# Twelve gathered table rows laid by VectorE, and the last tile's last three tables gathered in two halves

## The chip, the core and the metric

The kernel runs on one core of a Trainium2 chip. The metric is the device time of one execution in microseconds. Before the change it is 101.78 us, the median of three runs (101.72 to 101.84).

## The reference

A recommendation tower for 512 samples: 26 tables are looked up, all pairs of the 27 vectors (the dense one and 26 rows) are multiplied, and three layers follow.

```python
e = jnp.stack([tbl_0[ids[:, 0]], ..., tbl_25[ids[:, 25]]], axis=1)       # 512 x 26 x 128
combined = jnp.concatenate([dense_features[:, None, :], e], axis=1)      # 512 x 27 x 128
interactions = jnp.einsum('bnd,bmd->bnm', combined, combined)
z = jnp.concatenate([dense_features, interactions[:, _TRIU_I, _TRIU_J]], axis=1)
h = jnp.concatenate([z, dense_features], axis=1)                         # 512 x 607
h = jnp.maximum(h @ W_top1 + b_top1, 0.0)                                # 512 wide
h = jnp.maximum(h @ W_top2 + b_top2, 0.0)                                # 256 wide
y = h @ W_top3
```

## The kernel before

The samples are cut into four tiles of 128 (t = 0 to 3 in the code; the text counts tiles from 1). The kernel collects all 27 vectors of every sample in `xt`, with the 128 features on the partitions, `[128, sample/2, 27, 2]`.

Eleven small tables (1000 rows) are not gathered: TensorE multiplies them, in two parts, with a one-hot matrix that VectorE and ScalarE make (`lookup`, L339), and ScalarE copies the result to `xt`. This fills the first 47 us, beside the gathers.

The other fifteen tables are gathered by GpSimd: one indirect DMA fetches the rows of one table for the 128 samples of one tile into `rows_sb` (L312), samples on the partitions. Sixty such gathers follow one another, counted 0 to 59 here, fifteen a tile. `GROUPS` bundles them: four groups (4, 4, 4 and 3 tables) in each of tiles 1 to 3, and five (4, 4, 4, 2, 1) in tile 4, so groups 0 to 16. `rows_sb` holds two tiles; a gather of tile 3 or 4 waits until the group that had its place is turned (`FREED_BY`). Up to gather 42 every third one also waits for a lookup (L311), which keeps the gathers from running ahead.

When a group has landed, TensorE transposes its tables one by one into PSUM (`turn_group`, L354: a matrix product with the identity, 128 columns a table), and ScalarE copies the group to `xt` (`copy_group`, L697). Groups 0 to 7 are turned between the lookups (`AFTER_LOOKUP`), the others at places written out by hand in TensorE's program (L492 to L555).

Then, for each tile: `gram` (L376) makes the 27 x 27 products of each sample, in four quarters of 32 samples, `ps_gram`; `pack` on VectorE (L602, L607) transposes them in blocks of 32 and packs the triangle; `turn_z` (L387), ScalarE's `copy_z`, `layer1_dense` (L415) and `layer1_pairs` (L425), the ReLU on ScalarE (lower half, L720) and on VectorE (upper half, L638), `layer2` (L439), `layer3` (L468). The last tile has a version in chunks (`pack_last`, `turn_last_z`, `layer1_last_pairs` L402, `layer2_last`). TensorE's program mixes a tile's products with the layers of the tile before. `gram(3, 0)` waits until all groups are copied.

SyncE issues the loads: first the row numbers of all tiles for the gathers (`ids_sb`, L276), on which GpSimd's first gather waits, then tables and weights.

Of the kernel before, what the change touches and what calls it, by code (L numbers as in the profile page):

```python
# [15 lines left out]
P = 128  # L16
B = 512
# [60 lines left out]
assert all(sum(sizes) == len(GATHERED) for sizes in SIZES_OF_TILE)  # L78
FREED_BY = {g: max(e for e, (s, j, m) in enumerate(GROUPS) if s == t - ROWS_RING and j < i + k)
            for g, (t, i, k) in enumerate(GROUPS) if t >= ROWS_RING}  # L80

AFTER_LOOKUP = [[], [], [], [0], [1], [2], [3], [4], [5], [6], [7]]
LOOKED_UP_BESIDE = sum(len(gs) for gs in AFTER_LOOKUP)
assert sum(AFTER_LOOKUP, []) == list(range(LOOKED_UP_BESIDE)) and len(AFTER_LOOKUP) == FIRST_HALF_UP_TO
GROUPS_UP_TO = [sum(t <= tile for t, _, _ in GROUPS) for tile in range(TILES)]
# [41 lines left out]
def build(nc, dense_by_column, ids, ids_by_table, tables, w1, w2, columns, identity, out):  # L127
    with ExitStack() as ctx:  # L128
# [3 lines left out]
        def sem(name):  # L132
            return ctx.enter_context(nc.semaphore(name))
# [8 lines left out]
        ids_sb = sb("ids_sb", [P, TILES, F], I32)  # L142
        dense_sb = sb("dense_sb", [D, B], F32)
# [33 lines left out]

        ids_landed = sem("ids_landed")
        ident_landed = sem("ident_landed")
# [18 lines left out]
        group_copied = sem("group_copied")  # L198
        gram_done = sem("gram_done")
# [38 lines left out]

        def last_z(c):

            return ps_gram[:, c - 1, 0:P] if c else ps_z[:, 0, 0:P]
# [18 lines left out]
        def _(sp):  # L260
# [33 lines left out]
        def _(pool):  # L294
# [7 lines left out]
            pool.wait_ge(ids_landed, 16)  # L302
            for g, (t, first, n) in enumerate(GROUPS):
                if t >= ROWS_RING:
                    pool.wait_ge(group_turned, FREED_BY[g] + 1)
                for k in range(first, first + n):
                    f = GATHERED[k]
                    issued = t * len(GATHERED) + k
                    if issued >= GATHERS_AHEAD and (issued - GATHERS_AHEAD) % GATHERS_PER_LOOKUP == 0:
# [3 lines left out]
                        rows_sb[:, t % ROWS_RING, k, :], None, tables[f],  # L313
                        bass.IndirectOffsetOnAxis(ids_sb[:, t, f:f + 1], 0),
                    ).then_inc(group_landed[g], 16)

        @block.tensor
        def _(pe):
# [26 lines left out]
            def turn_group(g):  # L345

                t, first, n = GROUPS[g]
                if g >= 2:
                    pe.wait_ge(group_copied, g - 1)
                if g == 0:  # L350
                    pe.wait_ge(ident_landed, 16)
                pe.wait_ge(group_landed[g], 16 * n)
                for slot in range(n):
                    last = pe.transpose(ps_rows[:, g % 2, slot * P:(slot + 1) * P],  # L354
                                        rows_sb[:, t % ROWS_RING, first + slot, :], ident)
                last.then_inc(group_turned, 1)

            def gram(t, quarter):
# [4 lines left out]
                if quarter == 0:  # L363

                    pe.wait_ge(group_copied, GROUPS_UP_TO[t])
# [4 lines left out]
                    else:  # L370
                        pe.wait_ge(blocks_turned, t)
                for s in range(first, first + SPQ):
                    for j in range(P // NPAD):
                        b = t * P + j * NPAD + half * SPB + s
# [117 lines left out]
            turn_group(8)  # L492
# [4 lines left out]
            turn_group(9)  # L497
# [8 lines left out]
            layer2(0, 1)  # L506
            turn_group(10)
            turn_group(11)
# [7 lines left out]
            turn_group(12)  # L516
# [7 lines left out]
            turn_group(13)  # L524
# [3 lines left out]
            turn_group(14)  # L528
# [4 lines left out]
            turn_group(15)  # L533
            turn_group(16)
            layer1_pairs(2, 3)
            gram(3, 0)
            gram(3, 1)
            layer3([0, 1])
            layer2(2, 0)
            layer1_dense(3, 0)  # L540
# [106 lines left out]

# [178 lines left out]
```

## Time and profile before

| what | us |
|---|---|
| time, median of three runs | 101.78 |
| time of the profiled execution | 102.27 |
| its span, first to last instruction | 100.5 |
| TensorE busy (products) | 94.2 |
| VectorE busy | 52.6 |
| ScalarE busy | 50.6 |
| GpSimd busy | 61.3 |
| the sixty gathers, busy | 60.9 |

PE is TensorE's products, PEld its weight loads, DVE VectorE, ACT ScalarE, POOL GpSimd, SP SyncE. A gather's busy time on POOL is the time in which GpSimd issues it; its data land later. Times in the profile's answers are microseconds from the start of the span.

### The profile page before, as it was taken

To read this page: it belongs to the slowest core of one execution; us is meant where nothing else is said; L and a number is where in the kernel's file an instruction comes from. 1 tells how busy PE (TensorE), PEld (TensorE's weight loads), DVE (VectorE), ACT (ScalarE), POOL (GpSimd) and SP (SyncE) were. 2 spreads that over 40 slices of the span, in tenths; PEclk is the share of its full clock that TensorE was granted. 3 is DMA by queue.
4 is the path that set the end of the run, shared out by engine and by line. 5 is a ranking of instruction groups with operands and counts; after the bars stand their busy time and mean duration, and the time that the engine had idled before them with its cause. 6 is when DMAs were issued, how large, how long until landed. Compare 5 with 4: busy or idle time off the path is not lost.

```text
span 100.5 us, 3478 instructions
## 1 busy us (share of the span) xinstructions
PE 94.2 (94%) x1525; PEld 77.6 (77%) x1525; DVE 52.6 (52%) x117; ACT 50.6 (50%) x84; POOL 61.3 (61%) x66
## 2 busy tenths in 40 slices
PE   5999999999999999999999989999999897998990
PEld 1347788668888888899888878898898795987970
DVE  4599959999999969975000610262022601126020
ACT  2888999897499299384211242007400543003521
POOL 1488877777778877777777777777777760000000
PEclk9999999999999999999999999999999999999999
DMA  2999999999999999512222222212122221000000
GB/s 55 243 325 257 299 281 277 258 249 278 238 264 265 268 328 373 162 52 59 52 59 52 59 52 62 59 52 59 52 59 59 52 52 26 7 7 0 7 0 1
DMA packets 5366, 13.46 MB, mean 134 GB/s; under 512 B 1732, under 2 KB 1992, under 8 KB 5223
## 3 DMA queue, kind: packets, MB, share of 16 engines
q1 hardware_dynamic: 3260, 9.11, 33.0%
q0 software_dynamic: 1920, 3.94, 14.8%
q8 instruction: 12, 0.20, 0.9%
q10 hardware_dynamic: 170, 0.18, 0.8%
q14 instruction: 4, 0.02, 0.1%
HBM read 13.23 MB, written 0.00 MB: 132 GB/s over the span
## 4 chain that ended last, share of the span: by engine, by line
POOL 55%; issue 19%; PE 14%; DMA 8%; POOLq 1%; ACT 0%
POOL rows_sb L312 55%; DMA rows_sb<-tbl,ids_sb 5%; PE ps_a L402 3%; PE ps_gram L376 3%; DMA ids_sb<-ids 2%; PE ps_h L439 2%; PE ps_h L468 1%; POOLq L128 1%; PE ps_rows L451 1%; PE ps_rows L354 1%; PE ps_a L415 1%; PE ps_rows L456 1%; PE ps_a L425 1%; ACT y_sb L741 0%; PE ps_gram L395 0%
## 5 line engine op out<-in xcount | busy, mean ns | idle before, releaser
L312 POOL DMA_INDIRECT rows_sb<-tbl,ids_sb x60 | 60.9, 1015 | 20.4 <-issue 17.1
L339 PE MATMUL ps_a<-onehot,part_sb 125*128 125x512 f32 (+1 forms) x208 | 45.0, 366 | 0.4 <-ACT part_sb L668 0.2
L339 PEld LDWEIGHTS ps_a<-onehot,part_sb 125*128 125x128 f32 x208 | 34.1, 188 | 8.2 <-DVE onehot L575 1.2
L575 DVE TENSOR_SCALAR onehot<-idrow,row_id 125x1024 fp32r<-125x1024 int16 (+1 forms) x41 | 26.6, 708 | 1.5 <-DMA idrow<-ids_by_table 1.5
L584 DVE TENSOR_TENSOR part_sb<-table_sb,part_sb 125x512 fp32r<-125x512 f32 x22 | 14.4, 683 | 2.7 <-ACT part_sb L668 2.6
L690 ACT COPY xt<-ps_a 128x512 f32<-128x512 f32 (+1 forms) x13 | 7.6, 584 | 13.7 <-PE ps_a L339 13.5
L697 ACT COPY xt<-ps_rows 128x512 f32<-128x512 f32 (+3 forms) x17 | 9.9, 584 | 8.6 <-PE ps_rows L354 8.6
L376 PE MATMUL ps_gram<-xt 128*27 128x27 f32 x1024 | 13.4, 195 | 0.5 <-issue 0.2
L376 PEld LDWEIGHTS ps_gram<-xt 128*27 128x27 f32 x1024 | 11.1, 108 | 3.3 <-issue 0.6
L638 DVE TENSOR_SCALAR table_sb<-ps_a,columns_sb 128x128 f32<-128x128 f32 x8 | 2.4, 346 | 20.4 <-PE ps_a L425 17.3
L668 ACT CAST part_sb<-table_sb 125x1024 fp32r<-125x1024 f32 (+1 forms) x12 | 11.7, 979 | 0.6 <-DMA table_sb<-tbl 0.6
L602 DVE STREAM_TRANSPOSE table_sb<-ps_gram 128x864 f32<-128x864 f32 x3 | 3.3, 1084 | 13.7 <-PE ps_gram L376 13.7
L354 PE MATMUL ps_rows<-ident_sb,rows_sb 128*128 128x128 f32 x60 | 9.3, 274 | 1.2 <-DMA rows_sb<-tbl,ids_sb 1.2
L425 PE MATMUL ps_a<-table_sb,w_sb 128*128 128x128 f32 x72 | 9.4, 280 | 0.2 <-ACT table_sb L704 0.2
L354 PEld LDWEIGHTS ps_rows<-ident_sb,rows_sb 128*128 128x128 f32 x60 | 7.1, 141 | 2.4 <-ACT xt L697 1.0
L425 PEld LDWEIGHTS ps_a<-table_sb,w_sb 128*128 128x128 f32 x72 | 8.5, 192 | 0.5 <-issue 0.4
L679 ACT ACTIVATE distance<-idrow,row_id 125x1024 f32<-125x1024 int16 (+1 forms) x7 | 7.7, 1094 | 0.3 <-DMA idrow<-ids_by_table 0.3
L684 ACT ACTIVATE onehot<-distance 125x1024 fp32r<-125x1024 f32 (+1 forms) x7 | 7.0, 1001 | 0.5
L439 PE MATMUL ps_h<-table_sb,w_sb 128*128 128x128 f32 x48 | 6.9, 288 | 0.0
L439 PEld LDWEIGHTS ps_h<-table_sb,w_sb 128*128 128x128 f32 x48 | 5.8, 191 | 0.4 <-issue 0.2
L476 PE MATMUL ps_z<-zeros 128*128 128x512 bf16 x13 | 4.6, 529 | 1.2 <-DVE zeros L559 1.2
L736 ACT ACTIVATE table_sb<-ps_h,columns_sb 128x128 f32<-128x128 f32 x6 | 1.9, 373 | 5.6 <-PE ps_h L439 5.6
(41 smaller groups left out, 43.3 us busy)
## 6 DMA issues: line engine op xcount, KB each, us to landing
table_sb<-tbl SPq DMA_DIRECT2D x11, 448.0 KB
idrow<-ids_by_table SPq DMA_DIRECT2D x5, 256.0 KB, 7.5
w_sb<-w SPq DMA_DIRECT2D x1, 1280.0 KB, 9.9
rows_sb<-tbl,ids_sb POOLq DMA_INDIRECT x60, 5.7
table_sb<-tbl SPq DMA_DIRECT2D x10, 52.0 KB
w_sb<-w SPq DMA_DIRECT2D x1, 512.0 KB, 9.6
dense_sb<-dense_by_column SPq DMA_DIRECT2D x1, 256.0 KB, 7.6
idrow<-ids_by_table ACTq DMA_DIRECT2D x1, 128.0 KB, 2.8
```

The source lines that it names most:

```text
L312: pool.indirect_dma_start(rows_sb[:, t % ROWS_RING, k, :], None, tables[f], bass.IndirectOffsetOnAxis(ids_sb[:, t, f:f + 1], 0),).then_inc ...
L339: last = pe.matmul(ps_a[:, i % 2, a:b], parts_sb[part][:, w, c * D:(c + 1) * D], unit_onehot(u, c)[:, member, a:b], start=(part == HIGH an ...
L354: last = pe.transpose(ps_rows[:, g % 2, slot * P:(slot + 1) * P], rows_sb[:, t % ROWS_RING, first + slot, :], ident)
L376: last = pe.matmul(ps_gram[j * NPAD:j * NPAD + N, half, s * N:(s + 1) * N], x, x, start=True, stop=True)
L425: last = pe.matmul(h1_block(t, m), w1_sb[:, c, m * P:(m + 1) * P], zt[:, t % 2, c, :], start=False, stop=(c == ZC - 1), skip_group_check=True)
L439: last = pe.matmul(h2_block(t, m), w2_sb[:, k, m * P:(m + 1) * P], h1[:, t % 2, k, :], start=(k == 0 and m == 0), stop=(k == M1 - 1), skip ...
L575: dve.tensor_scalar(unit_onehot(u, c), idrow[0:VP, w, 0:n, :], row_id[0:VP, first + c:first + c + 1], None, ALU.is_equal).then_inc(onehot_ ...
L584: dve.tensor_tensor(parts_sb[LOW][:, w, columns], table_sb[0:VP, s, columns], parts_sb[HIGH][:, w, columns].bitcast(F32), ALU.subtract).th ...
L668: act.copy(parts_sb[HIGH][:, w, first:end], table_sb[0:VP, s, first:end]).then_inc(part_ready[HIGH], 1)
L679: act.activation(distance[:, 0:n, :], idrow[0:VP, w, 0:n, :], ACT.Abs, bias=row_id[0:VP, negated:negated + 1]) \
L690: act.copy(xt[:, a // RUN:b // RUN, 1 + h, :], ps_a[:, i % 2, a:b].rearrange("p (q r) -> p q r", r=RUN)).then_inc(lookup_copied, 1)
L697: act.copy(xt[:, t * P // RUN:(t + 1) * P // RUN, slots, :].rearrange("p q n r -> p n q r"), ps_rows[:, g % 2, 0:n * P].rearrange("p (n q ...
```

## The change

Three parts. **Laying:** tile 2 (code t = 1) is now bundled 4, 3, 8 and tile 4 again 4, 4, 4, 3. Two groups, `LAID`, are not turned by TensorE: group 6 (the last eight tables of tile 2) and group 11 (the first four of tile 4) are transposed by VectorE from `rows_sb` straight into `xt`, in 32 x 32 blocks, sixteen instructions each (`lay_group`). Twelve tables leave TensorE and ScalarE. **Halves:** the last three tables of tile 4 are gathered for its first 64 samples (group 14, three gathers of 64 rows) and then for the other 64 (group 15, three more, with their row numbers in a tensor of their own, and into rows of `rows_sb` that group 7 leaves free). `gram` of the last tile takes the first 64 samples in quarters 0 and 1, the others in quarters 2 and 3, and `copy_last_z` puts the samples back in order. TensorE's program at the end is written in another order. **Row numbers:** those of tile 1 are loaded first, the rest in a second transfer. Groups in after number 0 to 15.

```diff
-LAST_GROUP_SIZES = [4, 4, 4, 2, 1]
-SIZES_OF_TILE = [GROUP_SIZES] * (TILES - 1) + [LAST_GROUP_SIZES]
+SIZES_OF_TILE = [GROUP_SIZES, [4, 3, 8], GROUP_SIZES, GROUP_SIZES]
...
+HALF_TILE = P // 2
+FIRST_HALVES = len(GROUPS) - 1
+SECOND_HALVES = len(GROUPS)
+GROUPS.append(GROUPS[FIRST_HALVES])
+HALVED = GATHERED[-GROUP_SIZES[-1]:]
+FREES_ROWS = 7
...
-AFTER_LOOKUP = [[], [], [], [0], [1], [2], [3], [4], [5], [6], [7]]
+AFTER_LOOKUP = [[], [], [], [0], [1], [2], [3], [4], [5], [], []]
+LAID = [6, 11]
+TURNED = [g for g in range(len(GROUPS)) if g not in LAID]
...
-            sp.dma_start(ids_sb[:, :, :], ids).then_inc(ids_landed, 16)
+            sp.dma_start(ids_sb[:, 0, :], ids[:, 0, :]).then_inc(first_ids_landed, 16)
             load_first_table(sp, 0, VP_A)
+            sp.dma_start(ids_sb[:, 1:, :], ids[:, 1:, :]).then_inc(ids_landed, 16)
...
             sp.dma_start(ident_sb[:, :], identity).then_inc(ident_landed, 16)
+            sp.dma_start(second_ids_sb[:, :], second_ids).then_inc(second_ids_landed, 16)
...
                 if t >= ROWS_RING:
-                    pool.wait_ge(group_turned, FREED_BY[g] + 1)
+                    if FREED_BY[g] in LAID:
+                        pool.wait_ge(group_laid, LAID.index(FREED_BY[g]) + 1)
+                    else:
+                        pool.wait_ge(group_turned, TURNED.index(FREED_BY[g]) + 1)
...
+            pool.wait_ge(second_ids_landed, 16)
+            pool.wait_ge(group_turned, TURNED.index(FREES_ROWS) + 1)
+            for k, f in enumerate(HALVED):
+                pool.indirect_dma_start(
+                    rows_of(SECOND_HALVES)[:, k, :], None, tables[f],
+                    bass.IndirectOffsetOnAxis(second_ids_sb[:, k:k + 1], 0),
+                ).then_inc(group_landed[SECOND_HALVES], 16)
...
-                    pe.wait_ge(group_copied, GROUPS_UP_TO[t])
+                    pe.wait_ge(group_copied, TURNED_UP_TO[t] - (t == TILES - 1))
+                    if LAID_UP_TO[t]:
+                        pe.wait_ge(group_laid, LAID_UP_TO[t])
...
+                if t == TILES - 1 and quarter == QUARTERS // 2:
+                    pe.wait_ge(group_copied, TURNED_UP_TO[t])
...
+                        if t == TILES - 1:
+                            b = t * P + half * HALF_TILE + j * SPB + s
...
+            def lay_group(g, quarters=range(4)):
+
+                t, first, n = GROUPS[g]
+                slots = slice(FIRST_GATHERED + first, FIRST_GATHERED + first + n)
+                if 0 in quarters:
+                    dve.wait_ge(group_landed[g], 16 * n)
+                for a in (BLOCK * quarter for quarter in quarters):
+                    samples = slice((t * P + a) // RUN, (t * P + a + BLOCK) // RUN)
+                    for d in range(0, D, BLOCK):
+                        last = dve.transpose(
+                            xt[d:d + BLOCK, samples, slots, :].rearrange("p q n r -> p n q r"),
+                            rows_sb[a:a + BLOCK, t % ROWS_RING, first:first + n, d:d + BLOCK])
+                if 3 in quarters:
+                    last.then_inc(group_laid, 1)
+
+            lay_group(6)
             pack(0)
             relu1_high(0)
             pack(1)
+            lay_group(11, [0, 1, 2])
             relu1_high(1)
+            lay_group(11, [3])
             pack(2)
...
-                act.copy(zt[:, (TILES - 1) % 2, c, :], last_z(c)).then_inc(last_copied, 1)
+                act.copy(zt[:, (TILES - 1) % 2, c, :].rearrange("p (h j s) -> p h j s", h=2, s=SPB),
+                         last_z(c).rearrange("p (j h s) -> p h j s", h=2, s=SPB)).then_inc(last_copied, 1)
```

On TensorE, around the last tile's first products, before (L354 is `turn_group`, L425 `layer1_pairs`, L376 `gram`, L468 `layer3`, L439 `layer2`, L415 `layer1_dense`; a row is a run of equal instructions):

```order
L354 MATMUL ps_rows<-ident_sb,rows_sb 128x128 [waits group_landed15,group_copied]
L354 MATMUL ps_rows<-ident_sb,rows_sb 128x128
L354 MATMUL ps_rows<-ident_sb,rows_sb 128x128 [waits group_landed16,group_copied]
L425 MATMUL ps_a<-table_sb,w_sb 128x128 x3
L376 MATMUL ps_gram<-xt 27x27 [waits blocks_turned,lookup_copied,group_copied]
L376 MATMUL ps_gram<-xt 27x27 x63
L468 MATMUL ps_h<-table_sb,columns_sb 1x128 [waits h2_ready]
L468 MATMUL ps_h<-table_sb,columns_sb 1x128 x3
L439 MATMUL ps_h<-table_sb,w_sb 128x128 [waits h1_low_ready,h2_ready,layers_landed]
L439 MATMUL ps_h<-table_sb,w_sb 128x128 x3
L415 MATMUL ps_a<-dense_sb,w1d 128x128 [waits h1_low_ready]
L415 MATMUL ps_a<-dense_sb,w1d 128x128
```

and after (the same functions; L397 is `turn_group`, L475 `layer1_pairs`, L426 `gram`, L518 `layer3`, L465 `layer1_dense`, L489 `layer2`):

```order
L397 MATMUL ps_rows<-ident_sb,rows_sb 128x64 [waits group_landed14,group_copied]
L397 MATMUL ps_rows<-ident_sb,rows_sb 128x64 x2
L475 MATMUL ps_a<-table_sb,w_sb 128x128 x3
L426 MATMUL ps_gram<-xt 27x27 [waits lookup_copied,blocks_turned,group_laid,group_copied]
L426 MATMUL ps_gram<-xt 27x27 x31
L518 MATMUL ps_h<-table_sb,columns_sb 1x128 [waits h2_ready]
L518 MATMUL ps_h<-table_sb,columns_sb 1x128 x3
L465 MATMUL ps_a<-dense_sb,w1d 128x128 [waits h1_low_ready]
L465 MATMUL ps_a<-dense_sb,w1d 128x128
L426 MATMUL ps_gram<-xt 27x27 x32
L397 MATMUL ps_rows<-ident_sb,rows_sb 128x64 [waits group_landed15,group_copied]
L397 MATMUL ps_rows<-ident_sb,rows_sb 128x64 x2
```

Before, the products wait for both last groups; now they wait for the first halves, and the second halves are turned after half of the products; layer 2 and then the other two quarters stand behind that.

On GpSimd, the end of the gathers before:

```order
L312 DMA rows_sb<-tbl_16,ids_sb 128x128
L312 DMA rows_sb<-tbl_18,ids_sb 128x128
L312 DMA rows_sb<-tbl_21,ids_sb 128x128 [waits lookup_done,group_turned]
L312 DMA rows_sb<-tbl_22,ids_sb 128x128
L312 DMA rows_sb<-tbl_23,ids_sb 128x128 [waits group_turned]
```

and after:

```order
L345 DMA rows_sb<-tbl_18,ids_sb 128x128
L345 DMA rows_sb<-tbl_21,ids_sb 64x128 [waits lookup_done,group_laid]
L345 DMA rows_sb<-tbl_22,ids_sb 64x128
L345 DMA rows_sb<-tbl_23,ids_sb 64x128
L352 DMA rows_sb<-tbl_21,second_ids_sb 64x128 [waits group_turned,second_ids_landed]
L352 DMA rows_sb<-tbl_22,second_ids_sb 64x128
L352 DMA rows_sb<-tbl_23,second_ids_sb 64x128
```

Three gathers of 128 rows have become six of 64, the first three of which hold the first halves of all three tables.

## Rows read from the trace of the kernel before

**Rows 1.** The page, parts 1 and 2: busy us, share of span; granted TensorE clock.

```profile
PE 94.2 (94%) x1525; PEld 77.6 (77%) x1525; DVE 52.6 (52%) x117; ACT 50.6 (50%) x84; POOL 61.3 (61%) x66
...
PEclk9999999999999999999999999999999999999999
```

**Rows 2.** The page, part 4: the chain that ended last, by engine.

```profile
POOL 55%; issue 19%; PE 14%; DMA 8%; POOLq 1%; ACT 0%
```

**Rows 3.** That chain in order of time: start us, us, what.

```profile
0.74 2.49 DMA ids_sb<-ids
...
6.53 1.99 POOL rows_sb L312
...
43.63 0.96 POOL rows_sb L312
...
57.67 0.95 POOL rows_sb L312
...
77.68 2.68 DMA rows_sb<-tbl,ids_sb
...
81.43 2.53 DMA rows_sb<-tbl,ids_sb
```

**Rows 4.** Gathers on GpSimd: the page's group (mean ns), one late in time.

```profile
L312 POOL DMA_INDIRECT rows_sb<-tbl,ids_sb x60 | 60.9, 1015 | 20.4 <-issue 17.1
...
78.93 0.95 POOL L312 DMA_INDIRECT rows_sb<-tbl,ids_sb  x1 [0.30 <-PE ps_rows L354]
```

**Rows 5.** Waits of TensorE: who for whom, us in total, times, longest.

```profile
PE ps_rows L354 <- DMA rows_sb<-tbl,ids_sb: 1.2, 2, 0.7
```

**Rows 6.** Timeline of TensorE, 80 to 90 us: start, us, what, [idle before, releaser].

```profile
80.49 0.63 PE L354 MATMUL ps_rows<-ident_sb,rows_sb 128*128 128x128 f32 x4 [0.43 <-DMA rows_sb<-tbl,ids_sb]
...
82.97 0.38 PE L354 MATMUL ps_rows<-ident_sb,rows_sb 128*128 128x128 f32 x2
84.09 0.30 PE L354 MATMUL ps_rows<-ident_sb,rows_sb 128*128 128x128 f32 x1 [0.74 <-DMA rows_sb<-tbl,ids_sb]
...
84.99 1.25 PE L376 MATMUL ps_gram<-xt 128*27 128x27 f32 x126
...
86.61 1.16 PE L439 MATMUL ps_h<-table_sb,w_sb 128*128 128x128 f32 x8
87.61 0.61 PE L415 MATMUL ps_a<-dense_sb,w1d 128*128 128x128 f32 x4
88.15 1.53 PE L376 MATMUL ps_gram<-xt 128*27 128x27 f32 x128
89.61 1.16 PE L439 MATMUL ps_h<-table_sb,w_sb 128*128 128x128 f32 x8
```

**Rows 7.** Timeline of TensorE, 47 to 49 us.

```profile
47.41 0.49 PE L354 MATMUL ps_rows<-ident_sb,rows_sb 128*128 128x128 f32 x3
47.65 1.20 PE L339 MATMUL ps_a<-onehot,part_sb 125*128 125x256 f32 x8
```

**Rows 8.** Groups by line and shape: xcount, busy us, mean ns, idle before.

```profile
L620 DVE STREAM_TRANSPOSE table_sb<-ps_gram 128x672 f32<-128x672 f32 x1 | 0.9, 874 | 0.0
...
L620 DVE STREAM_TRANSPOSE table_sb<-ps_gram 128x192 f32<-128x192 f32 x1 | 0.4, 384 | 4.0 <-PE ps_gram L376 4.0
...
L298 POOL IOTA row_id<- 128x8 f32 x1 | 0.1, 133 | 0.4 <-POOLq L804 0.4
```

**Rows 9.** Timeline of VectorE, 45 to 80 us.

```profile
56.02 1.08 DVE L602 STREAM_TRANSPOSE table_sb<-ps_gram 128x864 f32<-128x864 f32 x1 [9.49 <-PE ps_gram L376]
...
74.63 0.61 DVE L638 TENSOR_SCALAR table_sb<-ps_a,columns_sb 128x128 f32<-128x128 f32 x2 [6.30 <-PE ps_a L425]
77.32 1.08 DVE L602 STREAM_TRANSPOSE table_sb<-ps_gram 128x864 f32<-128x864 f32 x1 [2.07 <-PE ps_gram L376]
```

**Rows 10.** DMA issues: xcount, KB each, median us from issue to landing.

```profile
idrow<-ids_by_table ACTq DMA_DIRECT2D x1, 128.0 KB, 2.8
ids_sb<-ids SPq DMA_DIRECT2D x1, 52.0 KB, 2.5
```

More of the change, by code:

```diff
@@ L74 @@
 GROUP_SIZES = [4, 4, 4, 3]
[L75 to L76 removed]
+SIZES_OF_TILE = [GROUP_SIZES, [4, 3, 8], GROUP_SIZES, GROUP_SIZES]
 GROUPS = [(t, sum(sizes[:i]), k) for t, sizes in enumerate(SIZES_OF_TILE) for i, k in enumerate(sizes)]
 assert all(sum(sizes) == len(GATHERED) for sizes in SIZES_OF_TILE)
+HALF_TILE = P // 2
[4 more added lines that the diff above has]
+FREES_ROWS = 7
+assert GROUPS[FREES_ROWS][:2] == (TILES - 2, 0) and GROUPS[FREES_ROWS][2] >= len(HALVED)
 FREED_BY = {g: max(e for e, (s, j, m) in enumerate(GROUPS) if s == t - ROWS_RING and j < i + k)
             for g, (t, i, k) in enumerate(GROUPS) if t >= ROWS_RING}
[L82 to L85 removed]
+AFTER_LOOKUP = [[], [], [], [0], [1], [2], [3], [4], [5], [], []]
+assert len(AFTER_LOOKUP) == FIRST_HALF_UP_TO
+LAID = [6, 11]
+TURNED = [g for g in range(len(GROUPS)) if g not in LAID]
+TURNED_UP_TO = [sum(GROUPS[g][0] <= tile for g in TURNED) for tile in range(TILES)]
+LAID_UP_TO = [sum(GROUPS[g][0] <= tile for g in LAID) for tile in range(TILES)]
+BLOCK = 32
 WARM_UP = 13
@@ L124, in packed_w1, with build @@
     return np.ascontiguousarray(np.stack(chunks, axis=1))
[L127 removed]
+def build(nc, dense_by_column, ids, second_ids, ids_by_table, tables, w1, w2, columns, identity, out):
     with ExitStack() as ctx:
@@ L237, in h2_block, with rows_of, samples_of @@
             return ps_h2[:, 0, m * P:(m + 1) * P]
+        def rows_of(g):
+            t, first, n = GROUPS[g]
+            if g == SECOND_HALVES:
+                return rows_sb[0:HALF_TILE, (t - 1) % ROWS_RING, 0:n, :]
+            return rows_sb[0:HALF_TILE if g == FIRST_HALVES else P, t % ROWS_RING, first:first + n, :]
+        def samples_of(g):
+            t = GROUPS[g][0]
+            middle = t * P + HALF_TILE
+            return (middle if g == SECOND_HALVES else t * P), (middle if g == FIRST_HALVES else (t + 1) * P)
         def last_z(c):
@@ L347, in turn_group @@
                 t, first, n = GROUPS[g]
-                if g >= 2:
-                    pe.wait_ge(group_copied, g - 1)
-                if g == 0:
+                place = TURNED.index(g)
+                if place >= 2:
+                    pe.wait_ge(group_copied, place - 1)
+                if place == 0:
                     pe.wait_ge(ident_landed, 16)
                 pe.wait_ge(group_landed[g], 16 * n)
+                first_sample, end = samples_of(g)
+                w = end - first_sample
                 for slot in range(n):
-                    last = pe.transpose(ps_rows[:, g % 2, slot * P:(slot + 1) * P],
-                                        rows_sb[:, t % ROWS_RING, first + slot, :], ident)
+                    last = pe.transpose(ps_rows[:, place % 2, slot * w:(slot + 1) * w],
+                                        rows_of(g)[:, slot, :], ident_sb[0:w, 0:w])
                 last.then_inc(group_turned, 1)
@@ L695, in copy_group @@
                 slots = slice(FIRST_GATHERED + first, FIRST_GATHERED + first + n)
-                act.wait_ge(group_turned, g + 1)
-                act.copy(xt[:, t * P // RUN:(t + 1) * P // RUN, slots, :].rearrange("p q n r -> p n q r"),
-                         ps_rows[:, g % 2, 0:n * P].rearrange("p (n q r) -> p n q r", n=n, r=RUN)).then_inc(group_copied, 1)
+                place = TURNED.index(g)
+                act.wait_ge(group_turned, place + 1)
+                first_sample, end = samples_of(g)
+                act.copy(xt[:, first_sample // RUN:end // RUN, slots, :].rearrange("p q n r -> p n q r"),
+                         ps_rows[:, place % 2, 0:n * (end - first_sample)].rearrange("p (n q r) -> p n q r", n=n, r=RUN)) \
+                   .then_inc(group_copied, 1)
             def copy_z(t):
@@ L821 @@
     out = nc.dram_tensor("y", (B, 1), F32, kind="ExternalOutput").ap()
-    build(nc, a["dense_by_column"], a["ids"], a["ids_by_table"], [a[f"tbl_{f}"] for f in range(F)],
+    build(nc, a["dense_by_column"], a["ids"], a["second_ids"], a["ids_by_table"], [a[f"tbl_{f}"] for f in range(F)],
           a["w1"], a["w2"], a["columns"], a["identity"], out)
```

54 lines of the change are left out of this document (31 added, 23 removed).

## The prediction

> **What bounds the kernel now.** I read the page's busy shares first: TensorE 94%, GpSimd 61%, with the granted clock at full speed in every slice [rows 1]. A busy TensorE is not yet a bound, so I read the chain that ended last: 55% of it is GpSimd's gathers and 19% "issue", which here is mostly the 0.30 us between two gathers [rows 2]. In order of time the chain starts with the load of the row numbers (0.74 to 3.23 us), passes through one gather after the other, and leaves GpSimd only at the last ones: the gather started at 77.68 lands 2.68 us later, the last, started at 81.43, lands at 83.96 [rows 3]. The period late in the kernel is 1.25 us (0.95 busy, 0.30 gap) [rows 4]. TensorE waits for gathered rows only twice, 1.2 us in all [rows 5]: 0.43 us before group 14 at 80.49, 0.74 us before group 16 at 84.09 [rows 6]. So the two engines are nearly level, GpSimd a little later, and it decides when the last tile's products can begin.
>
> For readers of the groups: gathers are counted 0 to 59, fifteen a tile; gathers 53 to 56 are group 14 of before, 57 and 58 group 15, 59 group 16. Group names of after are said as such.
>
> **Twelve rows laid by VectorE: TensorE's side.** TensorE loses twelve 128-column transposes: eight of tile 2 (code's t = 1), seen between the lookups, and four of tile 4. Three of them take 47.41 to 47.65, 0.08 us each [rows 7], so twelve are 1.0 us. Nearly all of that comes ahead of group 14's place. There TensorE already waits 0.43 us for gather 56, whose issue nothing in this edit hastens: the 1.0 us becomes waiting, 1.4 us in place of 0.43, and is worth **0** by itself. What it buys is 1.4 us of cover for any delay earlier on. ScalarE also loses three copies, off the path.
>
> **VectorE's side.** The laying is 16 transposes of 32 x 256 and 16 of 32 x 128. The same operation took 384 ns for 192 elements a partition and 874 for 672 [rows 8], 1.02 ns an element, so 0.45 us and 0.32 us each: 7.2 and 5.1 us. Both read and write SBUF where those rows read PSUM, so they bound it only roughly; 0.38 us for the shorter and 0.87 for the longer are the ends I keep. The first batch waits for gather 29, started at 43.63 [rows 3] and landed about 46.3 (2.66 us, as the last one), and so ends near 53.5. Queued behind it is the packing of tile 1, which before starts at 56.02 [rows 9] and now, after eight fewer transposes, at about 55.4. Cover 1.9 us, cost **0**; TensorE's products of tile 2, which newly wait for the laying, come after that packing anyway. The second batch waits for gather 48 (nine periods before 78.93, so 67.7; landed 70.3). Twelve of its sixteen end at 74.1. Behind them stands the ReLU of tile 2's upper half, at 74.63 before and now wanted at about 73.6: 0.5 us late, which the 1.4 us in front of group 14's place takes up. The last four end near 76.0, ahead of the packing of tile 3 at 77.32 less 1.0 [rows 9]. Cost **0**. GpSimd has new waits on the first batch before gathers 49, 53 and 57, the first of them 15 us after its end. If the laying slows the gathers it overlaps, that goes straight on the chain: over the whole run a gather took 1.015 us on average against 0.95 late [rows 4], so about nine gathers at 0.07 us are the upper end, 0.6 us. I take **0**, since the gather beside VectorE's packing of tile 1, started at 57.67, is busy 0.95 us as any late one [rows 3].
>
> **The first row numbers.** SyncE loads tile 1's numbers, 13 KB in place of 52, and the rest in a second transfer, which the gathers need only at gather 15. Of the loads at the same moment, 52 KB took 2.5 us and 128 KB 2.8 [rows 10]: 0.004 us a KB, so 39 KB less is **-0.15 us** (ends 0 and -0.2, no bytes at all). It shifts every gather, if the slow ones at the start (1.99 us for the third [rows 3]) do not move with it. SyncE's two extra issues precede waits that it makes anyway: 0.
>
> **The halves.** Gathers 57 to 59 become three gathers of 64 rows, and three more follow them. Let such a gather be busy h us, x = 0.95 - h less than a full one. No row shows h: all sixty gathers have 128 rows. The ends are 0.95 (the count does not matter) and 0.47 (all of it goes by rows). GpSimd's own row for a tiny instruction is 0.13 us [rows 8]; with that as the fixed part h is 0.54. I take **h = 0.65**, nearer that row than the upper end, as a gather must do more at its start than write numbers.
> The first halves land 3x earlier than gather 59 does now, so group 14 of after can be turned at 84.09 - 3x; but not before TensorE has done its 18 matmuls, now at 82.97 [rows 6]. With x = 0.30 that is 83.19: **-0.9 us**.
> On the other side, products start about 0.05 us later behind that point (three turned pieces are copied rather than one), the second halves add three 64-column transposes, up to 0.25 us, and the work between is cut up once more, 0.1: **+0.4 us**. The rest of the tail, from 84.99 to 89.61 and on, is the same work [rows 6].
> Whether TensorE then waits for the second halves: the last starts five periods after 78.93 and lands 2.66 - x after its start, with the semaphore at 87.84 - 6x. TensorE gets there 0.95 us after turning the first halves plus two quarters of products and layer 3 (84.99 to 86.61) and a dense step (87.61 to 88.15), so at 87.2 - 3x. The wait is 0.65 - 3x where positive (x = 0: 0.65): with x = 0.30, **0**, by 0.25 us. The copy of that last piece lies under layer 2.
>
> **Sum.** -0.15 - 0.9 + 0.4 = -0.65 us. The profiled execution has a span of 100.5 us and a time of 102.27, 0.49 over the median; all that moves lies within the span, so I put the change on the median: 101.78 - 0.65 = 101.1 us.
>
> By rows, then, everything hangs on h: the change is -0.15 - 3x + 0.4 + max(0, 0.65 - 3x), which is zero at x = 0.15, h = 0.80, and over 0.2 us of gain needs h under 0.77. (0.2%, 0.2 us, is about what a measurement of this kernel can tell from no change.)
>
> **Rivals.**
> (B) *A half gather costs a whole one.* Place: GpSimd's last six issues. Price: x = 0, so -0.15 + 0.4 + 0.65 = +0.9, 102.7 us, slower; it decides from h above 0.83. For it: the 0.30 us gap comes with every gather, and no row shows the busy time going by rows. Against: 0.95 us is far over the 0.13 of a small GpSimd instruction. The Trainium skill, "DMA: Bandwidth & Descriptors", section "Anatomy of one DMA", speaks for this rival: it calls descriptor generation small and variable, and says that "You can emit a lot of descriptors before the incremental cost shows up", so by it half the rows would save next to nothing and the sum would be this rival's; no run of before shows a second size to test it on.
> (C) *The laying is late.* If the transposes of SBUF rows take 0.87 us each, the first batch ends at 60.2, 4.8 us after the packing of tile 1 wants VectorE; less the 1.4 us of cover, the tail is some 3.4 us late: about 104.5, slower. It decides from 0.66 us each (9.1 us to the packing plus 1.4 of cover, over 16). Against: the slope of the two rows.
> (D) *The laying slows the gathers, or h is 0.77 to 0.83.* Up to 0.6 us of the gain is given back: 101.6 to 101.9, no difference.
> (E) *The halves go by rows alone.* h = 0.47: TensorE's own 18 matmuls then set the start, 84.09 - 82.97 = 1.1, so -0.2 - 1.1 + 0.4 = -0.9, 100.9; with the tail at 0.1 in place of 0.4 and a luckier start, 100.5.
>
> **How the numbers follow.** The forecast (h 0.53 to 0.77) 0.55, E 0.05: faster 0.60. D 0.13: within 0.2%. B 0.21 and C 0.06: slower 0.27. The time is the likeliest case's, 101.1; its own range is 100.8 to 101.6. The range for 8 in 10 reaches from E's 100.5 to 102.6, most of the way to B; C and the worst of B and D are left out.
>
> **What would show it.** In the profile after: the six 64-row gathers' busy time, near 0.65 us (B: 0.95); the first gather starting 0.15 us earlier; TensorE's wait for group 13 of after (gathers 53 to 56) grown to about 1.4 us while its start stays at about 80.3; its turn of the first halves at 83.0; no wait, or a slight one, at the second halves; 32 more VectorE transposes of 0.45 and 0.32 us, the first batch over by 54 us; late gathers still at a 1.25 us period. The forecast is wrong if the half gathers keep 0.9 us, if VectorE's packing of tile 1 starts after 56 us, or if the gathers between 47 and 54 us stretch.

## The result and the profile after

The change makes the kernel **slower**: 102.69 us (median of 20 runs) against 101.9 us for the kernel before (20 runs beside them), a ratio of 1.0072 with a 95% interval of 1.0051 to 1.0094. The change run again (E10) gave 1.0123 (1.0079 to 1.0167). The forecast was 101.1 us and faster; the time lies outside its range, next to rival B (102.7). The profiled execution of after has a span of 100.9 us and a time of 102.7, where before has 100.5 and 102.27. Some executions of most kernels here take over 1.5% longer than the same kernel's fastest; the ratios leave them out, and the profiles of E3, E7, E12, E15 and E16, taken in such executions, are not read.

The page of after, parts 1 and 2 (busy us, share, instructions; granted clock) and 4 (the chain that ended last), answering [rows 1, 2], and from part 5 the gathers and the laying (busy us, mean ns, idle before):

```profile
PE 93.4 (93%) x1516; PEld 77.1 (76%) x1516; DVE 64.4 (64%) x149; ACT 48.9 (48%) x81; POOL 63.6 (63%) x69
...
PEclk9999999999999999999999999999999999999999
...
PE 43%; POOL 21%; issue 11%; DMA 11%; DVE 7%; ACT 3%; POOLq 1%; SPq 1%; DVEq 0%
...
L345 POOL DMA_INDIRECT rows_sb<-tbl,ids_sb x60 | 60.5, 1008 | 20.2 <-issue 17.4
...
L706 DVE STREAM_TRANSPOSE xt<-rows_sb 32x256 f32<-32x256 f32 (+1 forms) x32 | 11.9, 371 | 2.2 <-DMA rows_sb<-tbl,ids_sb 1.8
```

GpSimd is 2.3 us busier: three gathers more, and the row of sixty, three of which now fetch 64 rows only, has hardly shrunk. Its timeline says why (start, us, what):

```profile
77.12 0.95 POOL L345 DMA_INDIRECT rows_sb<-tbl,ids_sb  x1 [0.30 <-issue]
78.38 0.90 POOL L345 DMA_INDIRECT rows_sb<-tbl,ids_sb  x1 [0.30 <-issue]
...
84.40 0.91 POOL L352 DMA_INDIRECT rows_sb<-tbl,second_ids_sb  x1 [0.30 <-issue]
```

A gather of 128 rows is busy 0.95 us, one of 64 rows 0.90. The prediction took 0.65. The chain of GpSimd is 0.55 us ahead at the first half gather (78.38, before 78.93 [rows 4]); in E10's execution of the same kernel it was 0.32 ahead.

TensorE's timeline for the same stretch as [rows 6] (start, us, what, idle before and its end):

```profile
83.20 0.37 PE L397 MATMUL ps_rows<-ident_sb,rows_sb 64*128 64x64 f32 x3 [0.64 <-DMA rows_sb<-tbl,ids_sb]
...
84.36 0.95 PE L426 MATMUL ps_gram<-xt 128*27 128x27 f32 x62
...
86.32 0.75 PE L426 MATMUL ps_gram<-xt 128*27 128x27 f32 x64
88.15 0.37 PE L397 MATMUL ps_rows<-ident_sb,rows_sb 64*128 64x64 f32 x3 [1.08 <-DMA rows_sb<-tbl,second_ids_sb]
88.44 1.16 PE L489 MATMUL ps_h<-table_sb,w_sb 128*128 128x128 f32 x8
89.53 1.28 PE L426 MATMUL ps_gram<-xt 128*27 128x27 f32 x128
90.74 1.16 PE L489 MATMUL ps_h<-table_sb,w_sb 128*128 128x128 f32 x8
```

The last tile's products begin 0.63 us earlier (84.36; before 84.99), as hoped. Then TensorE waits 1.08 us for the second halves and turns them in 0.29, and layer 2's second half, the last step of the tail that both kernels share, starts at 90.74 in place of 89.61: 1.13 us late. From 84.36 to there after takes 6.38 us, before 4.62; of these 1.76 us, 1.37 are that wait and that turn, and the other 0.39 are put down to the work being cut up once more, which no run shows alone. The spans differ by 0.4 us only, because before takes 0.7 us more behind that point (10.9 to the end of the span, after 10.2). TensorE's timeline there, first before's, which is not shown ahead of the prediction, then after's:

```profile
91.25 0.38 PE L402 MATMUL ps_a<-table_sb,w_sb 128*128 128x128 f32 x1
92.08 0.60 PE L402 MATMUL ps_a<-table_sb,w_sb 128*128 128x128 f32 x3 [0.45 <-issue]
...
95.21 1.16 PE L451 MATMUL ps_rows<-table_sb,w_sb 128*128 128x128 f32 x8
```

```profile
92.39 0.71 PE L452 MATMUL ps_a<-table_sb,w_sb 128*128 128x128 f32 x4
...
95.62 1.16 PE L501 MATMUL ps_rows<-table_sb,w_sb 128*128 128x128 f32 x8
```

Before, TensorE stops for 0.45 us in the middle of a run of four products, with nothing named that it waits for. From the first of these four to the next layer (L451, after L501) before takes 3.96 us and after 3.23, so this place accounts for the 0.7 us. After has no such gap there, but more of them among the products; TensorE's waits of after, first row:

```profile
PE ps_gram L426 <- issue: 1.7, 3, 0.8
```

These gaps turned out to matter as much as anything in the change.

### The profile page after: what moved, and what is told of

Read it like the earlier page. It is cut to its first block, busy times and chain, and to the rows that moved or that the text cites. A ratio compares the mean times of both kernels' runs of the same rounds, so it can differ in the third digit from the quotient of the medians.

```text
span 100.9 us, 3496 instructions
## 1 busy us (share of the span) xinstructions
PE 93.4 (93%) x1516; PEld 77.1 (76%) x1516; DVE 64.4 (64%) x149; ACT 48.9 (48%) x81; POOL 63.6 (63%) x69
## 4 chain that ended last, share of the span: by engine, by line
PE 43%; POOL 21%; issue 11%; DMA 11%; DVE 7%; ACT 3%; POOLq 1%; SPq 1%; DVEq 0%
PE ps_a L379 28%; POOL rows_sb L345 19%; DMA table_sb<-tbl 5%; DVE onehot L624 5%; DMA rows_sb<-tbl,second_ids_sb 4%; PE ps_gram L426 3%; PE ps_a L452 3%; PE ps_rows L397 3%; DMA idrow<-ids_by_table 3%; PE ps_h L489 2%; DVE part_sb L633 2%; POOL rows_sb L352 2%; POOLq L137 1%; PE ps_rows L501 1%; ACT distance L746 1%
## 5 line engine op out<-in xcount | busy, mean ns | idle before, releaser
L379 PE MATMUL ps_a<-onehot,part_sb 125*128 125x512 f32 (+1 forms) x208 | 44.4, 367 | 0.2 <-DVE onehot L624 0.2
L426 PE MATMUL ps_gram<-xt 128*27 128x27 f32 x1024 | 13.2, 194 | 1.8 <-issue 1.7
L426 PEld LDWEIGHTS ps_gram<-xt 128*27 128x27 f32 x1024 | 11.0, 107 | 4.4 <-issue 2.0
L766 ACT COPY xt<-ps_rows 128x512 f32<-128x512 f32 (+2 forms) x14 | 8.0, 570 | 13.0 <-PE ps_rows L397 13.0
L706 DVE STREAM_TRANSPOSE xt<-rows_sb 32x256 f32<-32x256 f32 (+1 forms) x32 | 11.9, 371 | 2.2 <-DMA rows_sb<-tbl,ids_sb 1.8
L475 PE MATMUL ps_a<-table_sb,w_sb 128*128 128x128 f32 x72 | 9.6, 283 | 0.2 <-ACT table_sb L774 0.2
L397 PE MATMUL ps_rows<-ident_sb,rows_sb 128*128 128x128 f32 (+1 forms) x51 | 7.5, 269 | 1.7 <-DMA rows_sb<-tbl,second_ids_sb 1.1
L475 PEld LDWEIGHTS ps_a<-table_sb,w_sb 128*128 128x128 f32 x72 | 8.5, 191 | 0.8 <-issue 0.4
L397 PEld LDWEIGHTS ps_rows<-ident_sb,rows_sb 128*128 128x128 f32 (+1 forms) x51 | 5.9, 140 | 3.0 <-issue 2.2
L489 PE MATMUL ps_h<-table_sb,w_sb 128*128 128x128 f32 x48 | 7.0, 288 | 0.0
L526 PE MATMUL ps_z<-zeros 128*128 128x512 bf16 x13 | 5.7, 632 | 1.2 <-DVE zeros L608 1.2
L489 PEld LDWEIGHTS ps_h<-table_sb,w_sb 128*128 128x128 f32 x48 | 5.8, 191 | 0.2
```

Source lines behind the costliest of these rows:

```text
L379: last = pe.matmul(ps_a[:, i % 2, a:b], parts_sb[part][:, w, c * D:(c + 1) * D], unit_onehot(u, c)[:, member, a:b], start=(part == HIGH an ...
L397: last = pe.transpose(ps_rows[:, place % 2, slot * w:(slot + 1) * w], rows_of(g)[:, slot, :], ident_sb[0:w, 0:w])
L426: last = pe.matmul(ps_gram[j * NPAD:j * NPAD + N, half, s * N:(s + 1) * N], x, x, start=True, stop=True)
L475: last = pe.matmul(h1_block(t, m), w1_sb[:, c, m * P:(m + 1) * P], zt[:, t % 2, c, :], start=False, stop=(c == ZC - 1), skip_group_check=True)
L489: last = pe.matmul(h2_block(t, m), w2_sb[:, k, m * P:(m + 1) * P], h1[:, t % 2, k, :], start=(k == 0 and m == 0), stop=(k == M1 - 1), skip ...
L706: last = dve.transpose(xt[d:d + BLOCK, samples, slots, :].rearrange("p q n r -> p n q r"), rows_sb[a:a + BLOCK, t % ROWS_RING, first:first ...
```

## The experiments

Ratios are to runs of the kernel before beside them on the same chip, with the 95% interval.

**The parts one by one.** E1 is the change without halves, its tail in the order of before; E2 the halves alone, every group turned by TensorE and one load of row numbers; E3 the kernel before with the split load alone; E4 the laying alone, which is E1 with one load. The first two lines are E1's, the next two E2's, the rest E3's (and, the other way round, E4's):

```diff
-SIZES_OF_TILE = [GROUP_SIZES, [4, 3, 8], GROUP_SIZES, GROUP_SIZES]
+SIZES_OF_TILE = [GROUP_SIZES, [4, 3, 8], GROUP_SIZES, [4, 4, 4, 2, 1]]
...
-LAID = [6, 11]
+LAID = []
...
-sp.dma_start(ids_sb[:, :, :], ids).then_inc(ids_landed, 16)
+sp.dma_start(ids_sb[:, 0, :], ids[:, 0, :]).then_inc(first_ids_landed, 16)
+sp.dma_start(ids_sb[:, 1:, :], ids[:, 1:, :]).then_inc(ids_landed, 16)
```

> The change without the halves: twelve rows laid by VectorE and the row numbers split, but tile 4's last three tables gathered for all 128 samples (groups of 2 and 1), TensorE's tail in the order of before. Theory S (the six half gathers, 0.90 us each, are the loss): 0.2 to 0.5 us faster than before, since the gathers start 0.27 us earlier and nothing else is added. Theory F (TensorE's instruction fetches, seen as 16 KB packets of the instruction queue, delay the last landing by chance of place): as fast as before or faster, 101.4 to 101.9. Theory L (the laying itself costs, TensorE's gaps named issue, 1.7 us in after against 0.2): slower than before by about as much as the change, 0.5 us or more.

> Before with the halves alone (all other groups turned by TensorE, row numbers in one load). Theory S: 0.6 to 0.9 us slower than before, with TensorE waiting 0.5 to 1 us for the second halves. Theory F: the fetches fall elsewhere against the gathers, so the last landing is 2.3 us and not 3.6, the wait at the second halves is gone and the kernel is within 0.4 us of before. Theory L: no difference from before or faster.

> Before with the row numbers of tile 1 loaded first, alone. My sum said -0.15 us, the trace of the change shows the first gather 0.27 us earlier: 0.1 to 0.3 us faster. If the slow first gathers only wait for something else: no difference.

> Before with the laying alone (row numbers in one load, groups of 2 and 1 at the end). My sum: no difference, as TensorE's saving becomes waiting for gathers; theory S and F the same, within 0.2 us of before. Theory L: slower by 0.3 us or more.

Measured: without halves 0.9944 (0.9904 to 0.9984); halves alone 1.0055 (1.0011 to 1.01); row numbers alone 0.9995 (0.9952 to 1.0038); laying alone 0.9899 (0.9832 to 0.9966). So the halves cost time with and without the laying, the row numbers bring nothing that can be measured, and the laying seemed to gain 0.6 to 1.0%, where the prediction had put it at nothing. Halves alone show after's wait; their TensorE timeline:

```profile
88.04 0.37 PE L394 MATMUL ps_rows<-ident_sb,rows_sb 64*128 64x64 f32 x3 [0.95 <-DMA rows_sb<-tbl,second_ids_sb]
```

**The price of a gather by its rows.** E5 cuts the three first halves to 32 rows and the three second ones to 16 (the rows left out keep what an earlier gather put there):

```diff
+rows = 32 if g == FIRST_HALVES else P
-rows_of(g)[:, k - first, :], None, tables[f],
+rows_of(g)[0:rows, k - first, :], None, tables[f],
...
-rows_of(SECOND_HALVES)[:, k, :], None, tables[f],
+rows_of(SECOND_HALVES)[0:16, k, :], None, tables[f],
```

> The disputed cost by itself: the changed kernel with the first three half gathers cut to 32 rows and the other three to 16 (the other rows of those samples are left out). Theory S1 (nearly all of a gather's busy time is fixed, 0.945 us at 128 rows and 0.90 at 64 give 0.7 ns a row): about 0.88 us at 32 and 0.87 at 16. My working (fixed 0.13, the rest by rows) would have said 0.33 and 0.23; a step at 128 rows alone would give 0.90 for both.

GpSimd's timeline, with 128, 32 and 16 rows:

```profile
79.26 0.95 POOL L346 DMA_INDIRECT rows_sb<-tbl,ids_sb  x1 [0.30 <-issue]
80.51 0.87 POOL L346 DMA_INDIRECT rows_sb<-tbl,ids_sb  x1 [0.30 <-issue]
...
86.33 0.84 POOL L353 DMA_INDIRECT rows_sb<-tbl,second_ids_sb  x1 [0.30 <-issue]
```

From 128 rows to 16 the busy time falls by 0.11 us, about 1 ns a row over some 0.83 us that every gather pays, and the 0.30 us gap stays. The small price of a row agrees with the sentence of the Trainium skill ("DMA: Bandwidth & Descriptors", "Anatomy of one DMA") that the prediction quoted for rival B.

**Why the second halves come late.** TensorE reaches them at 87.07. The last gather starts at 84.40; landing like its two neighbours (2.3 to 2.4 us) it would be there by 86.8. It took 3.61 us. After's chain in order of time, and the DMA queues of 85.4 to 86.0 us (packets, MB, share of 16 engines):

```profile
84.40 3.61 DMA rows_sb<-tbl,second_ids_sb
```

```profile
q8 instruction: 1, 0.02, 12.4%
```

In that flight falls a 16 KB packet of instructions. My theory: it holds up a part of the gather. E7 (32 samples' products) and E8 (48, otherwise the same) put more of TensorE's work ahead, so that the packet and the gather would not meet.

```diff
+for i in range(32):
+    x = xt[:, i, :, 0]
+    pe.matmul(ps_gram[i % 4 * NPAD:i % 4 * NPAD + N, 0, 0:N], x, x, start=True, stop=True)
 turn_group(14)
```

> The changed kernel with 64 extra weight loads and 64 extra products ahead of the turn of the first halves, where TensorE waits 0.64 us, so that the 16 KB instruction fetch behind them comes 128 instructions earlier in the program. Theory F (the fetch at 85.6 us holds up the last half gather, 3.6 us to land against 2.3): the fetch starts by about 85 us, the last gather lands in 2.3 to 2.8 us, TensorE's wait at the second halves falls from 1.1 to 0.5 us or less, and the time falls by 0.3 to 0.8 us against the change, ratio to before 1.000 to 1.005. Theory S (issue time alone): the wait stays near 1 us, ratio 1.007 or above.

> As the run with 128 instructions, with 192 (96 loads and 96 products, some 0.8 us, of which 0.64 lie in the wait). Theory F: the fetch is over before the last half gather's data move, that gather lands in 2.3 us, no wait at the second halves; 0.2 us of the extra work shows; ratio to before 0.998 to 1.004. Theory S: wait as before, ratio 1.007 to 1.01.

Measured: 1.0137 (1.004 to 1.0235) and 1.012 (1.0032 to 1.0209). The wait for the second halves was gone in E8's profile, but no time came back; its TensorE timeline shows a new gap instead:

```profile
91.03 0.82 PE L426 MATMUL ps_gram<-xt 128*27 128x27 f32 x73 [0.94 <-issue]
```

As a test of the packet these two failed: the edit moved the gaps as well. The change run again (E10, below) tells more. Its profiled execution was the quickest of its runs (102.13 us, span 100.3). TensorE was later there and the packet came at 86.5, when the gather was nearly home. It landed in 2.5 us at most (the gathers' row of landing times), and TensorE did not wait (its timeline):

```profile
DMA to landing us min/median/max: 2.3/2.4/2.5
```

```profile
86.88 0.74 PE L426 MATMUL ps_gram<-xt 128*27 128x27 f32 x64
87.56 0.39 PE L397 MATMUL ps_rows<-ident_sb,rows_sb 64*128 64x64 f32 x3
...
90.17 1.05 PE L489 MATMUL ps_h<-table_sb,w_sb 128*128 128x128 f32 x7
```

Layer 2's second half starts 0.57 us earlier than in the other profile, and the span is 0.6 shorter. So whether packet and gather meet fits the difference between two executions of one kernel; that the packet causes the delay is argued from these landings. More landings bear it out. In the fifteen profiles read here, 117 gathers that start after 50 us have a landing in the trace. The 51 with no packet in their flight all took 2.6 us or less; the 13 in whose flight a packet began 1.0 to 1.6 us after the gather's start all took 3.2 to 3.7 us. Still, no run moved the packet alone.

**Taking the second halves away.** E9 leaves out the three gathers and TensorE's wait for them (the rows of tile 3 stand in; TensorE makes the same products and turns in the same order), with the change (E10) beside it. E14 leaves out their turn and copy as well (zeros stand in):

```diff
-pool.wait_ge(second_ids_landed, 16)
-pool.wait_ge(group_turned, TURNED.index(FREES_ROWS) + 1)
-for k, f in enumerate(HALVED):
-    pool.indirect_dma_start(
-        rows_of(SECOND_HALVES)[:, k, :], None, tables[f],
...
-turn_group(15)
...
-copy_group(15)
```

> The changed kernel without the three gathers of the second halves (left out: those samples' rows of three tables, tile 3's rows stand in; TensorE turns them without a wait). All of TensorE's, ScalarE's and VectorE's work and order stays. Theory S (the loss is that six issues of 0.90 us bring the second halves late): TensorE has no wait there, the time is 0.5 to 1.1 us below the change and below before, about as without the halves. If the loss lies in the tail's extra transposes and order, the time stays at the change's, 0.4 to 0.8 us above before.

> The change itself again, beside the others on one chip: 0.5 to 0.9% slower than before, TensorE waiting about 1 us for the second halves where it comes in time for them, less where waits for tables among the lookups have made it late.

> The change without the second halves altogether: no second gathers, and no turn and copy of them either (zeros, written by VectorE at the start in about 0.2 us, stand in their place). Against the kernel that left out the gathers only (1.0023 of before): if the turn of the second halves and its place between the products cost the 0.6%, 0.995 to 0.997; if not, 1.000 to 1.003.

Measured: E9 1.0023 (0.9984 to 1.0062) beside 1.0123 (1.0079 to 1.0167) for the change, so the three extra gathers and the wait for them cost 1.0%. The forecast had E9 below before; it came out level with it, so this is not the whole loss against the kernels without halves. E14 0.9952 (0.9915 to 0.9989). E14's TensorE timeline, to lay beside that of after:

```profile
83.47 0.37 PE L391 MATMUL ps_rows<-ident_sb,rows_sb 64*128 64x64 f32 x3 [0.70 <-DMA rows_sb<-tbl,ids_sb]
...
86.36 0.75 PE L418 MATMUL ps_gram<-xt 128*27 128x27 f32 x64
87.04 1.16 PE L481 MATMUL ps_h<-table_sb,w_sb 128*128 128x128 f32 x8
...
89.33 1.16 PE L481 MATMUL ps_h<-table_sb,w_sb 128*128 128x128 f32 x8
```

From the same quarter of products (86.36; after 86.32) layer 2's second half follows 2.97 us later, in after 4.42: 1.45 us, the wait and the turn. And even with the second halves for nothing, the kernel is no quicker than one without halves.

**The order of the tail.** E6 and E16 are one kernel: whole gathers with the change's order of work and of samples, the last three tables in one group. E13 is that with the last tables in groups of 2 and 1 again (the last pair of lines). E11 and E15 are E1 again.

```diff
-FIRST_HALVES = len(GROUPS) - 1
-SECOND_HALVES = len(GROUPS)
-GROUPS.append(GROUPS[FIRST_HALVES])
+FIRST_HALVES = SECOND_HALVES = None
...
-turn_group(15)
...
-SIZES_OF_TILE = [GROUP_SIZES, [4, 3, 8], GROUP_SIZES, GROUP_SIZES]
+SIZES_OF_TILE = [GROUP_SIZES, [4, 3, 8], GROUP_SIZES, [4, 4, 4, 2, 1]]
```

> The changed kernel without the split of the gathers: tile 4's last three tables in three gathers of 128 rows, turned once, but TensorE's tail and the sample order as in the change. If the loss is the six issues and the landing of the second halves: 0.2 to 0.8 us faster than before, like the change without the halves (ratio 0.994). If the new order of the tail or the strided copies cost it: slower than before, like the change (ratio 1.007).

> The change without the halves, again: 0.3 to 0.9% faster than before, so 1.0 to 1.6% below the change on the same chip.

> The order of the change (layer 3, then a dense step, then the second quarter of products; its order of samples; its wider copies), whole gathers, the last group bundled 2 and 1 as in the kernel before. If the order or the copies cost the 0.6%: 1.001 to 1.004 of before, as the kernel with a last group of three was (1.0034). If they cost nothing: 0.994 to 0.996, as the kernel without halves.

> The change without halves, order and bundles of before at the end, a third time, beside the others: 0.994 to 0.997 of before by every theory.

> The order of the change with whole gathers and a last group of three, again. If the group of three costs the 0.6% (all three tables turned after the last gather, three copied in one piece): 1.001 to 1.004, with the kernel of 2 and 1 below it. If neither: 0.994 to 0.997, and the earlier 1.0034 was spread (0.9972 to 1.0096).

Measured: E6 1.0034 (0.9972 to 1.0096), unclear; E11 0.9964 (0.9928 to 1.0001); E13 0.9946 (0.9909 to 0.9984); E15 0.996 (0.9915 to 1.0004); E16 0.9933 (0.9887 to 0.9978, on six of its runs). Neither order, bundles nor copies cost anything that these runs can tell. The loss is in the second halves.

**More laying.** E12 is E4 with a third group laid, the second four tables of tile 3:

```diff
-LAID = [6, 11]
+LAID = [6, 8, 11]
```

> The laying alone (row numbers in one load, no halves), with a third batch for VectorE: the second group of tile 3 (four tables, 16 transposes of 0.32 us, 5.1 us in an idle stretch of 5.2 us between 58 and 63 us). If TensorE's saving counts because TensorE is often later than the gathers (0.35 us for four transposes more): 1.0 to 1.3% faster than before. If GpSimd sets the end in most runs: as the laying alone, 0.5 to 1.0% faster. If the third batch holds up the ReLU behind it: slower than the laying alone.

Measured: 1.0 (0.996 to 1.004); with four more turns off TensorE nothing more was gained, which already spoke against TensorE's saved work as the cause of the gain.

**What the laying's gain is.** My theory by then was that TensorE, not GpSimd, sets the end in most executions, so that its saved 1.0 us counts. The rival was the gap: the profiles of before and of the halves alone have one behind the last products (0.45 and 0.48 us), those of the kernels with laying none there, and these have twelve turns fewer ahead of the place. Two kernels were to part them. E17 keeps the laying (E4) and makes twelve samples' products of tile 1 twice; E18 is the kernel before with twelve products left out. In both TensorE's work moves by only about 0.14 us. E17's lines, then E18's:

```diff
-for s in range(first, first + SPQ):
+for s in list(range(first, first + SPQ)) + ([0, 1, 2] if (t, quarter) == (0, 0) else []):
...
-for s in range(first, first + SPQ):
+for s in range(first + (3 if (t, quarter) == (0, 0) else 0), first + SPQ):
```

> The laying alone, with twelve samples' products of tile 1 made twice (12 weight loads and 12 products more, about 0.14 us of TensorE), so that TensorE's program has as many instructions behind it as in the kernel before. If the laying's gain is TensorE's saved work (1.0 us less 0.14): 0.990 to 0.996 of before, no gap in the layers behind the last products. If it is the place of the gaps: 0.998 to 1.002, with the gap of 0.2 to 0.5 us there again.

> The kernel before with twelve samples' products of tile 1 left out (12 loads and 12 products less, about 0.14 us of TensorE; these twelve samples' products stay zero). If the laying's gain is TensorE's saved work: 0.998 to 1.000 of before, gap in the tail as in before. If it is the place of the gaps: 0.993 to 0.996, and the gap of the tail gone.

Measured: the laying with twelve products more 1.0238 (1.0182 to 1.0294), outside both forecasts; the kernel before with twelve less 0.9946 (0.9905 to 0.9986), as forecast for the gap, where 0.14 us of work alone would make 0.9986. So the kernel before gets a gain like the laying's (0.9899 to 0.9964 in E1, E4, E11) from twelve products fewer, with no laying at all, and with twelve products more the laying loses it and 2.4% on top. TensorE's timelines around the place, with twelve more (first fence) and twelve less (second):

```profile
89.11 0.49 PE L471 MATMUL ps_h<-table_sb,w_sb 128*128 128x128 f32 x2
91.66 0.83 PE L471 MATMUL ps_h<-table_sb,w_sb 128*128 128x128 f32 x6 [2.05 <-issue]
```

```profile
91.13 0.71 PE L402 MATMUL ps_a<-table_sb,w_sb 128*128 128x128 f32 x4
91.68 0.27 PE L395 MATMUL ps_gram<-ident_sb,z 128*128 128x128 f32 x1
```

In the one a gap of 2.05 us opens inside layer 2; in the other the four products of L402, which before broke apart, run through.

This takes the ground from my theory, but does not refute it. E17's profiled execution took 103.25 us; less its gap it would stand at 101.2, still under the 101.9 of before. In E4's profile TensorE waits for no gathered row in the whole span, as the theory says. And E1, which gains as well, has a gap of its own among the last products:

```profile
88.70 1.06 PE L411 MATMUL ps_gram<-xt 128*27 128x27 f32 x102 [0.64 <-issue]
```

What the laying's gain is stays open. Shown is that moving the gaps by twelve products is worth as much as that gain, or more.

## Why the prediction was wrong

- **The halves, the price h: wrong.** 0.90 us in place of 0.65. The step that failed is the choice of h, taken near GpSimd's 0.13 us for a tiny instruction [rows 8], an instruction that issues no DMA; the upper end, a whole gather, was the nearer row. Rival B had the right price. With h at 0.90 (x = 0.05) the prediction's own formula gives -0.15 - 0.15 + 0.4 + 0.5 = +0.6 us; measured were +0.79 between the medians. That the two lie so near, and that B's 102.7 us was met, is in part luck: in the profile the terms came out otherwise, as the next four points say.
- **The first products earlier: right in time, for another reason.** The first halves were turned at 83.20 (forecast 83.19), 0.89 us earlier than before's last group. The cheap gathers gave 0.08 of that; 0.55 came from a chain further ahead (0.15 was forecast) and 0.26 from a shorter landing (2.27 us, before 2.53). E2, with neither the laying nor the split load, has its first half gather at 78.28, so being that far ahead need not come from the change.
- **The +0.4 us for the cutting up: too small.** From the turn of the first halves to the first products it took 1.16 us, before 0.90: 0.26 more, where 0.05 was forecast. The turn of the second halves cost 0.29 (0.25) and the cutting up 0.39 (0.1), 0.94 in all.
- **No wait for the second halves: wrong,** 1.08 us. This term was put at 0, and E9 beside the change shows 1.0% for it and the gathers behind it. It follows from h only in part. With h at 0.90 the formula has TensorE there at 87.05, the last gather's start at 84.93 and its data ready for TensorE at 87.54; measured were 87.07, 84.40 and 88.15. The gather started earlier, but from its start to the turn it took 3.75 us (3.61 to land) where the formula has 2.61, taken from a landing of before. With 2.61 there would have been no wait in this execution, and in E10's there was none. The wait needed both: five issues of 0.90 ahead, which start the last gather 1.25 us later than issues of 0.65 would, and the late landing.
- **The sum lacked a term:** the gap in before's tail, idle 0.45 us and worth 0.7, in the profile that the sum was made against. I read the chain of that profile as GpSimd's and TensorE's work alone; a row "issue" inside a run of products stood in the timeline for anyone who read on to 92 us.
- **Laying, TensorE's side worth 0: not settled.** E1, E4, E11 and E13 lie 0.4 to 1.0% below before and E12 level with it, while E18 shows a gain of that size without any laying. The working behind the 0 did not hold in after: no 1.4 us of waiting showed up before group 13, which TensorE turned at 79.74 without a wait. The gathers were ahead of the forecast, and gaps of 1.7 us stood among the products, against 1.0 us of turns saved.
- **Laying, VectorE's side: right.** After's VectorE timeline, to be read beside [rows 9]:

```profile
46.70 7.21 DVE L706 STREAM_TRANSPOSE xt<-rows_sb 32x256 f32<-32x256 f32 x16
55.70 1.08 DVE L651 STREAM_TRANSPOSE table_sb<-ps_gram 128x864 f32<-128x864 f32 x1 [1.79 <-PE ps_gram L426]
...
69.63 3.79 DVE L706 STREAM_TRANSPOSE xt<-rows_sb 32x128 f32<-32x128 f32 x12 [1.78 <-DMA rows_sb<-tbl,ids_sb]
74.44 0.61 DVE L687 TENSOR_SCALAR table_sb<-ps_a,columns_sb 128x128 f32<-128x128 f32 x2 [1.03 <-PE ps_a L475]
```

  7.21 us for sixteen and 3.79 for twelve are 0.45 and 0.32 each, as worked out; the first batch is over 1.79 us before the packing can start. Rivals C and D fell.
- **Row numbers:** the first gather starts 0.27 us earlier (3.24, before 3.51; forecast 0.15). E3 (0.9995) shows no gain, but its interval is too wide to exclude the 0.15 us.

What stays open: how the loss divides when the parts are added up. The second gathers cost 1.0% (E9 beside the change, TensorE's program the same), the rest of the halves' tail up to 0.7% (E9 to E14, which were not run beside each other), and the gap moved out of before's tail may give about 0.5% back (E18). Any edit that changes the number of TensorE's instructions also moves its gaps, so single parts cannot be weighed here to better than that. Nor was the packet kept away from the last gather without moving the gaps.

Kernels that beat both are those without halves: the laying alone (0.9899) or with the change's order (E13, 0.9946). By E18 a gain of this size can come from where the gaps fall alone, and it may go with the next edit.

## What to carry to other kernels

Before cutting a transfer into pieces so that work can begin sooner, price the issue, not the bytes: if the only evidence for a cheap half is an instruction of another kind, take the whole transfer's price, and ask what the later pieces make late. Before a gain of half a percent is put down to saved work, run a control that changes the instruction count by as much and the work by nothing, in both directions. And read the timeline of the bounding engine to the end of the span for idle time that has no releaser.

## What the runs showed of the hardware

The instruction queue q8 carries packets of 16 KB, twelve in a run; E8, whose TensorE has 192 instructions more, has thirteen, so they are taken to be TensorE's instructions. Before, over the whole span, and the window of 89 to 92 us with twelve products more (packets, MB, share of 16 engines):

```profile
q8 instruction: 12, 0.20, 0.9%
```

```profile
q8 instruction: 1, 0.02, 2.7%
```

That one packet occupied a DMA engine for 1.3 us (2.7% of 16 engines over 3 us) from 89.0 us on, and the gap of 2.05 us ends at 91.66. The gaps lie in or right behind stretches of many small products, and where they lie, and how long they are, changed with twelve products more or less ahead of them. In the fifteen profiles read here TensorE has 27 gaps of 0.3 us or more for which no releaser is named, and in every one the next product starts 1.25 to 1.60 us after the end of a packet. That ties the gaps to the packets. The Trainium skill ("Runtime: NRT & Kernel Launch", "Instruction fetch mechanics") says that instructions are refilled in blocks of 16 KiB and that crossing a boundary is "mostly hidden". The size agrees with the packets here; hidden it was not in this kernel, if these gaps are that refill. Which instruction each packet carries, no row shows.
